# The keys' normalisation moves from VectorE to GpSimd, and the keys' statistics get two turns of their small tile

## Time and profile before

| | |
|---|---|
| time, three runs | 1517.54 us median (1517.3 to 1518.57) |
| profiled execution, its own time | 1516.25 us |
| its span | 1514.6 us |
| TensorE busy | 1379.9 us, 91% |
| VectorE busy | 778.9 us, 51% |
| ScalarE busy | 582.1 us, 38% |
| GpSimd busy | 134.1 us, 9% |
| mean granted TensorE clock | 0.971 |

### The profile page before, as it was taken

How to read it: one execution, slowest core, us unless ns; L and a number is a source line. 1 busy time by engine, 2 the same in 40 slices (tenths; PEclk the granted TensorE clock), 3 DMA queues, 4 the chain that set the end, 5 groups by cost and what they waited for, 6 DMA issues and landing times.

```text
span 1514.6 us, 24316 instructions
## 1 busy us (share of the span) xinstructions
PE 1379.9 (91%) x7888; PEld 874.7 (58%) x7889; DVE 778.9 (51%) x1879; ACT 582.1 (38%) x1082; POOL 134.1 (9%) x184
## 2 busy tenths in 40 slices
PE   6888998989989989899895499999999999999997
PEld 5667676676766866767664244444444444444442
DVE  5765866858768678587556433222322222232225
ACT  3574655736556557365563012121111212121110
POOL 1000020110110200102002100000000000000005
PEclk9999999999999999999998599999999999999998
DMA  9783142141321422414215845360706064300005
GB/s 365 286 318 124 61 163 94 59 170 59 118 111 61 161 94 70 169 49 150 80 56 194 329 185 199 113 248 14 277 14 270 21 270 166 122 24 14 21 8 173
DMA packets 53566, 207.48 MB, mean 137 GB/s; under 512 B 4902, under 2 KB 5012, under 8 KB 47388
## 3 DMA queue, kind: packets, MB, share of 16 engines
q1 hardware_dynamic: 40320, 123.14, 22.4%
q0 software_dynamic: 13184, 83.89, 14.5%
q10 hardware_dynamic: 28, 0.01, 0.0%
HBM read 144.11 MB, written 62.91 MB: 137 GB/s over the span
## 4 chain that ended last, share of the span: by engine, by line
PE 72%; DVE 9%; issue 6%; ACT 6%; DMA 4%; POOL 1%; SPq 1%; DVEq 0%; ACTq 0%
PE bank L621 21%; PE bank L1439 8%; PE bank L1397 8%; PE bank L603 6%; PE bank L604 5%; PE bank L605 5%; DMA moe_w<-in_L_ffn_w_dram 3%; PE bank L613 3%; PE bank L1406 2%; PE bank L1487 2%; ACT moe_w L933 2%; PE bank L1465 2%; PE bank L1421 2%; DVE moe_w L1093 1%; PE bank L1440 1%
## 5 line engine op out<-in xcount | busy, mean ns | idle before, releaser
L621 PE MATMUL bank<-moe_w,arena 128*128 x736 | 330.9, 592 | 0.0
L489 DVE SCALAR_TENSOR_TENSOR arena<-bank,now_scales,arena 128x512 f32<-128x512 f32 x92 | 69.0, 750 | 346.5 <-PE bank L605 346.5
L1397 PE MATMUL bank<-moe_w 128*128 128x257 f32 x768 | 200.2, 400 | 30.1 <-DVE moe_w L867 30.1
L621 PEld LDWEIGHTS bank<-moe_w,arena 128*128 128x128 f32 x736 | 132.7, 190 | 132.5 <-issue 132.5
L426 ACT ACTIVATE arena<-arena 128x512 f32<-128x512 f32 x92 | 58.3, 633 | 338.2 <-DVE arena L489 338.2
L1397 PEld LDWEIGHTS bank<-moe_w 128*128 128x128 f32 x768 | 144.2, 200 | 51.3 <-DVE moe_w L867 26.2
L603 PE MATMUL bank<-moe_w,arena 128*128 x368 | 140.9, 383 | 2.5 <-DVE arena L502 2.3
L604 PE MATMUL bank<-moe_w,arena 128*128 x368 | 140.6, 382 | 0.0
L605 PE MATMUL bank<-moe_w,arena 128*128 x368 | 140.5, 382 | 0.0
L1439 PE MATMUL bank<-moe_w 128*128 128x512 f16 x384 | 114.4, 379 | 10.0 <-ACT moe_w L924 7.0
L910 ACT ACTIVATE moe_w<-bank,cols,ugain 128x512 f32<-128x512 f32 x96 | 74.6, 777 | 61.6 <-PE bank L1440 60.6
(11 more groups left out here) (224 smaller groups left out, 2121.3 us busy)
## 6 DMA issues: line engine op xcount, KB each, us to landing
moe_w<-w_halves POOLq DMA_DIRECT2D x8, 4096.0 KB, 13.2
moe_w<-in_L_ffn_w_dram POOLq DMA_DIRECT2D x8, 4096.0 KB, 24.4
w_halves<-moe_w SPq DMA_DIRECT2D x56, 512.0 KB, 3.4
moe_w<-in_L_ffn_w_dram SPq DMA_DIRECT2D x24, 1024.0 KB, 5.7
xs_rows<-blocks SPq DMA_DIRECT2D x8, 2048.0 KB, 13.0
arena<-in_ctx_dram SPq DMA_DIRECT2D x32, 384.0 KB
arena<-in_L_ffn_w_dram SPq DMA_DIRECT2D x8, 1024.0 KB, 4.9
arena<-in_L_ffn_b_dram POOLq DMA_DIRECT2D x8, 1024.0 KB, 25.7
```

The source lines that it names most:

```text
L489: nc.vector.scalar_tensor_tensor(out=h_sb[:, fb % 2, :], in0=bank[fb % 2][:, :], scalar=now_scales[:, KD:KD + 1], in1=b1_rows[:, bass.ds(s ...
L621: last = nc.tensor.matmul(Y[:, :], hT_sb[:, fb % 2, c, :], moe_flat[:, bass.ds((e % 2) * 16384 + 8192 + (4 * fb + c) * DIM, DIM)], start=( ...
L1397: last = nc.tensor.matmul(bank[h][:, 0:KEYS], qkT[:, c, b, h * P:(h + 1) * P], cnT[:, b % 2, c, :], start=(c == 0), stop=(c == KC - 1))
```

## The change

The three tensor_scalar instructions of cn_apply leave VectorE's stream and stand in GpSimd's, behind the power instruction. cn_pow now takes g and b. It waits for cn_var, and for cn_done of the batch before (its own earlier work, which reads crstd); makes the root; waits for its completion; runs a mark instruction (a one-column add into cn_mark); and then runs the three tensor_scalar, of which the last raises cn_done. cn_apply and its five calls are taken out of VectorE's stream. The small tile cmv has two turns, used by batch parity, so that VectorE can write the statistics of one batch while GpSimd still reads those of the one before; VectorE waits for cn_done of two batches back before it writes into a turn. The places of the statistics in VectorE's stream, and of the roots in GpSimd's, are unchanged.

```diff
--- before.py
+++ after.py
@@ -170,7 +170,7 @@
         rstd = sb("rstd", [P, 1])
         fin_mv = sb("fin_mv", [P, 2, 3])
         cstats = sb("cstats", [P, 3, 6])
-        cmv = sb("cmv", [P, 3, 2])
+        cmv = sb("cmv", [P, 2, 3, 2])
         crstd = sb("crstd", [P, 3])
         negm = sb("negm", [P, HG])
         rsum = sb("rsum", [P, HG])
@@ -241,6 +241,7 @@
         now_scales = sb("now_scales", [P, KD + 1])
         tiny = sb("tiny", [P, 1])
         heads_mark = sb("heads_mark", [P, 1])
+        cn_mark = sb("cn_mark", [P, 2])
         zero1 = sb("zero1", [P, 1])
         pool_mark = sb("pool_mark", [P, 1])
         dve_mark = sb("dve_mark", [P, 1])
@@ -284,7 +285,7 @@
         halves_out = [sem(f"halves_out{i}") for i in range(3)]
         sum_done, scale_done, w_high_done, w_low_done, heads_marked, heads_zero = sem("sum_done"), sem("scale_done"), sem("w_high_done"), sem("w_low_done"), sem("heads_marked"), sem("heads_zero")
         most_step, most_full, scales_ok, now_ok, xh_done = sem("most_step"), sem("most_full"), sem("scales_ok"), sem("now_ok"), sem("xh_done")
-        cmv_ok = sem("cmv_ok")
+        cmv_ok, cn_marked = sem("cmv_ok"), sem("cn_marked")
         slots_final = sem("slots_final")
         y2_free, rows_seen = sem("y2_free"), sem("rows_seen")
         rt_step, mask_done, exps_ready, gexp_done = sem("rt_step"), sem("mask_done"), sem("exps_ready"), sem("gexp_done")
@@ -777,10 +778,20 @@
                 pool.wait_ge(ln_var, n + 1)
                 nc.gpsimd.tensor_tensor(rstd[:, :], mv[:, 1:2], half[:, 0:1], ALU.pow).then_inc(ln_rstd, 1)
 
-            def cn_pow(n):
-
+            def cn_pow(g, b):
+
+                n, slot, turn = GB * g + b, b % GB, b % 2
                 pool.wait_ge(cn_var, n + 1)
-                nc.gpsimd.tensor_tensor(crstd[:, :], cmv[:, :, 1], half[:, 0:3], ALU.pow).then_inc(cn_rstd, 1)
+                if not isinstance(n, int) or n > 0:
+                    pool.wait_ge(cn_done, n)
+                nc.gpsimd.tensor_tensor(crstd[:, :], cmv[:, turn, :, 1], half[:, 0:3], ALU.pow).then_inc(cn_rstd, 1)
+                pool.wait_ge(cn_rstd, n + 1)
+                nc.gpsimd.tensor_tensor(cn_mark[:, turn:turn + 1], half[:, 0:1], half[:, 0:1], ALU.add).then_inc(cn_marked, 1)
+                for k in range(3):
+                    c = ctx[0:PART[k], slot, k, :]
+                    last = nc.gpsimd.tensor_scalar(c, c, cmv[0:PART[k], turn, k, 0:1], crstd[0:PART[k], k:k + 1],
+                                                   ALU.subtract, ALU.mult)
+                last.then_inc(cn_done, 1)
 
             def body(g, do_a, do_b, nxt):
                 ln = ln_before(g)
@@ -791,13 +802,13 @@
                 if do_b:
                     mark_free(g - 1)
                 if isinstance(g, int) and g == 0:
-                    cn_pow(2)
+                    cn_pow(0, 2)
                 if do_a:
-                    cn_pow(GB * g + 3)
+                    cn_pow(g, 3)
                 if nxt:
-                    cn_pow(GB * g + 4)
-                    cn_pow(GB * g + 5)
-                    cn_pow(GB * g + 6)
+                    cn_pow(g, 4)
+                    cn_pow(g, 5)
+                    cn_pow(g, 6)
                     ln_pow(ln + 1)
                     ln = ln + 2
                 if do_b:
@@ -832,8 +843,8 @@
 
             ln_pow(0)
             ln_pow(1)
-            cn_pow(0)
-            cn_pow(1)
+            cn_pow(0, 0)
+            cn_pow(0, 1)
             body(0, True, False, True)
             pool.wait_ge(xs_zeroed, 16 * (EXPERTS + 1))
             body(1, True, True, True)
@@ -1012,7 +1023,7 @@
         @block.vector
         def _(dve):
             nc.vector.memset(blocks[:, :, :], 0.0).then_inc(zeros_ok, 1)
-            nc.vector.memset(cmv[:, :, :], 1.0).then_inc(cmv_ok, 1)
+            nc.vector.memset(cmv[:, :, :, :], 1.0).then_inc(cmv_ok, 1)
             nc.vector.memset(dve_mark[:, :], 0.0).then_inc(b_free, 1)
             dve.wait_ge(cmv_ok, 1)
 
@@ -1047,21 +1058,12 @@
                     last = nc.vector.bn_stats(cstats[0:PART[k], k, :], ctx[0:PART[k], slot, k, :])
                 link = chain(dve, cn_step, 2 * bt)
                 link(last)
+                at_least(dve, cn_done, bt - 1)
                 carry_wait()
                 for k in range(3):
-                    last = nc.vector.bn_aggr(cmv[0:PART[k], k, :], cstats[0:PART[k], k, :])
+                    last = nc.vector.bn_aggr(cmv[0:PART[k], b % 2, k, :], cstats[0:PART[k], k, :])
                 link(last)
-                nc.vector.tensor_scalar(cmv[:, :, 1], cmv[:, :, 1], EPS, None, ALU.add).then_inc(cn_var, 1)
-
-            def cn_apply(g, b):
-
-                bt, slot = GB * g + b, b % GB
-                dve.wait_ge(cn_rstd, bt + 1)
-                for k in range(3):
-                    c = ctx[0:PART[k], slot, k, :]
-                    last = nc.vector.tensor_scalar(c, c, cmv[0:PART[k], k, 0:1], crstd[0:PART[k], k:k + 1],
-                                                   ALU.subtract, ALU.mult)
-                last.then_inc(cn_done, 1)
+                nc.vector.tensor_scalar(cmv[:, b % 2, :, 1], cmv[:, b % 2, :, 1], EPS, None, ALU.add).then_inc(cn_var, 1)
 
             def m_copy(g, at, dst, src):
                 dve.wait_ge(m_full, M_FILLS * g + at + 1)
@@ -1163,7 +1165,6 @@
                     for n in range(0, 16, 2):
                         setup_out(dve, nc.vector.tensor_copy, n)
                     cn_stats(0, 1)
-                    cn_apply(0, 1)
                 for i in range(QK_PAIRS):
                     if do_a:
                         qk_copy(dve, nc.vector.tensor_copy, g, i, 0)
@@ -1210,18 +1211,14 @@
                         cn_stats(g, b + 2)
                     if do_b and b == 0:
                         heads_apart(g - 1)
-                    if ahead:
-                        cn_apply(g, b + 2)
                     if isinstance(g, int) and g == 0 and b == 0:
                         cn_stats(0, 2)
-                        cn_apply(0, 2)
                     if do_b and b == 2:
                         ss_sub(g - 1)
                 if do_b and not do_a:
                     most_of()
                 if nxt:
                     cn_stats(g, 6)
-                    cn_apply(g, 6)
                 if do_a:
                     row_scales(g, 0, 2)
                 if nxt:
@@ -1314,7 +1311,6 @@
             xn_norm(0, 0, 0)
             xn_norm(1, 0, 1)
             cn_stats(0, 0)
-            cn_apply(0, 0)
             body(0, True, False, True)
             dve.wait_ge(gate_in, 32)
             dve.wait_ge(consts, 7)
```

## The result

The changed kernel takes 1573.82 us (median of 4) beside 1518.05 us for the kernel before (median of 4): a ratio of 1.0371, 95% interval 1.0353 to 1.0389, so 56 us slower where 3.7 us faster was forecast.

A forecast was written before the change was run, and what follows sets the result against it. TensorE, busy 91% of the span, was taken as the bound. Batch 1's 2.06 and batch 2's 1.67 us in group 0 sum to 3.7, steady groups 0: 1517.54 - 3.7 = 1513.8 us, range 1511.5 to 1516.5.

The forecast's parts named there:

- What bounds the kernel: Whole kernel: TensorE, busy 91% of the span; VectorE's saved work counts only where TensorE waits for it.
- Batch 1: Group 0, 30 to 36 us: the copy freeing a score bank starts earlier, so TensorE gains 2.06 of its 2.32 us wait.
- The part that is added: T: GpSimd's time for one moved normalising instruction of 384 columns, taken as 0.65 us from memset and affine select rows.
- Batch 2: Group 0, 52 to 58 us: TensorE's transposes of the keys start earlier, a gain of 1.67 us at T = 0.65.
- The formula 3.62 - 3T: Batch 2's gain in us at TensorE's key transposes, with T the time per GpSimd normalisation; at most 2.14.
- What stands behind the normalisation: GpSimd's in-order queue in a steady body: the layer norm root after six normalisations stays in time, so moved work costs nothing.
- The room, 0.99 us per normalisation: Steady bodies: the largest T at which the layer norm root behind six normalisations is still ready when VectorE wants it.
- rival (b): T above 0.99: layer norm root late by 6(T - 0.99) in seven bodies; 1524.3 us at T = 1.2; chance 0.10.
- The range: Whole kernel time from 1511.5 (a 6 us gain) to 1516.5 us (1 us gain), leaving out slower outcomes.
- The prediction's own sign of being wrong: Steady groups: the body's period changes, or a transposing L1406 or L778 waits for GpSimd.

The follow-up runs named there:

- e3: The changed kernel with sixteen one-column memsets ahead of VectorE's loop and batch 6's GpSimd work behind both layer norm roots: 1519.13 us, ratio 1.0016.
- the probe: The kernel before with 24 extra GpSimd instructions ahead of its first layer norm root, to time each form: 1.54 us for the normalisation's form on 352 columns.
- e10: The kernel before with nine unused GpSimd products between batch 6's root and the layer norm's root in groups 0 to 6: 1556.3 us, ratio 1.0256.
- e1: The changed kernel with sixteen one-column memsets on VectorE ahead of its loop: 1553.47 us, ratio 1.0247.
- e4: The kernel before with only the head of VectorE's loop moved to instruction slot 239: 1544.83 us, ratio 1.0175.
- e7: The kernel before with only the head of VectorE's loop put at instruction slot 0: 1519.02 us, ratio 1.0004.
- e2: The changed kernel with batch 6's GpSimd work moved behind both layer norm roots: 1544.97 us, ratio 1.019.

## Why the prediction was wrong

- **What bounds the kernel.** Right: VectorE's 39 us of less work bought nothing in the steady groups (e3's six turns from group 1 on are no shorter in sum than those of the kernel before).
- **Batch 1.** Right in mechanism and about in size: TensorE's whole 2.32 us went, where 2.06 was forecast.
- **The part that is added: T.** The failed step. I took 0.65 us between bounds of 0.34 and 0.86, from a memset and an affine select of the same engine, and left "the upper side open" while using the lower. It is 1.65, 2.5 times that. Neither row does arithmetic with two operations; the probe puts 1.09 for one with a constant, 1.17 with a scalar, 1.54 for two. The one row that did arithmetic on several columns, the root at 0.145 us a column, I had set aside. The Trainium skill (GPSIMD Engine Reference, section 3.1, Elementwise) gives VectorE about 1 cycle an element, GpSimd 2.6, and a ratio of 1.96 for a tensor_tensor of 2048 columns; by that ratio, an estimate, T was 0.93. But the moved instruction is no tensor_tensor: the trace has a ratio of 3.5 for its form, and the measurement decides.
- **Batch 2.** The formula 3.62 - 3T was right, and only T in it wrong: it gives -1.3 at T = 1.65, TensorE's transposes came about where it says (57.04 after a start 2.4 earlier), and the first o_proj product is 1.4 us later with both batches on GpSimd than with batch 1 alone. The medians of those two kernels are 3.7 us apart; where the rest comes from is open.
- **What stands behind the normalisation.** The room, 0.99 us per normalisation, was right: VectorE's wait for the root went from 0.67 to 4.5, and 6(1.65 - 0.99) is 4.0. This was rival (b), to which I gave 0.10. Its price was too small: it charges the lateness alone, which at T = 1.65 is 28 us for seven groups. e10 shows 5.6 us a group for 4.1 us more of TensorE's waiting (4.99 against 0.90), and its mean clock is 0.955 against 0.971: TensorE goes on at half clock after the wait.
- **The range** closed at 1516.5 though T's upper side was called open. A price without a row belongs in the range with all that it can do: (b)'s own sum gives 1524.3 at T = 1.2, and about 1544 at T = 1.65. The prediction's own sign of being wrong came true, since the five turns with a branch grew by 8 to 10 us and L779 waited on GpSimd's queue.
- **No step at all:** the change makes VectorE's program 16 slots shorter ahead of its loop and the loop 12 shorter, and the loop then fetches its start anew in each of 5 turns, with VectorE idle for some 5.8 us. e1 takes 20 us off with padding alone, and e4 brings the same gap into the kernel before by the loop's place alone. That the fetch waits behind the transfers that fill the DMA engines at that moment is argued from their share of about 1.0 in the gap's first half; no run tests it.

## What to carry to other kernels

Before moving work to an engine with an in-order queue, list what another engine awaits from that queue, and compare the moved time with the idle time ahead of each such item. Price it by a probe or by the worst row with the same kind of arithmetic, never by a memset. After any edit of a looped program, look at the packets of the instruction queue and at "issue" waits behind the loop's branch: a shorter program can make its loop fetch its start anew in every turn.

## What the runs showed of the hardware

- **A loop's place.** The same 279 instructions leave VectorE idle 0.3 us a turn at one head slot (the kernel before, 14 packets) and 6.6 us a turn at another (e4, 41 packets). The Trainium skill (Runtime: NRT & Kernel Launch, Instruction fetch mechanics) says that a taken branch to a target outside the current two blocks of 256 instructions forces a fetch before execution goes on; by that rule, the trace agrees, 279 instructions from slot 239 reach a third block, and the same from slot 0 (e7) do not and show no gap at the turns. The page gives no price for such a branch; here it was 5.8 us (changed kernel) and 6.6 us (e4) of VectorE's time.
- **The clock.** Where TensorE waits some 3 to 4 us longer in a turn, the stretch 400 to 500 us has some 10 us more at 1.2 GHz (0.93 against 0.98), for a late root (e1) as for a late loop start (e2, e4). Both waits in one turn cost little more clock than one (0.93 in that stretch, 0.949 over the whole kernel against 0.952 and 0.955).
- **GpSimd and VectorE.** VectorE's normalisation takes 2.62 in place of 1.25 us beside GpSimd's products, while its statistics (0.55 for one block) and its work out of PSUM (0.69) take the same beside the changed kernel's normalisations as alone. The other way round, three normalisations take 6.41 us beside VectorE's L1118 and what follows it (e3) against 4.92:

```profile
300.81 6.41 POOL L793 TENSOR_SCALAR arena<-arena,cmv,crstd 128x384 f32<-128x384 f32 x3
```

```profile
301.73 2.34 DVE L1118 SCALAR_TENSOR_TENSOR moe_w<-moe_w,row_scale 128x2048 f16<-128x2048 f32 x1
```

The Trainium skill (Advanced Engine Details and Errata, Miscellaneous Facts, GPSIMD Details) names a possible cause, a read and a write interface that the two share, with conflicts when VectorE runs in a two-port mode or reads two inputs from SBUF. By that rule, the trace agrees for L1118, which reads two SBUF inputs, and for the operations on PSUM, which didn't slow; whether the normalisation ran in a two-port mode no view shows.
